# A reordered front of a fused attention kernel: index rows, corner tables and first one-hots

## The chip, the cores and the metric

The kernel runs on one core of a Trainium2 chip. The metric is the device time of one execution in microseconds (us); a smaller number is better. Engines are named as the profile names them: PE (TensorE matmul) and PEld (its weight load), DVE (VectorE), ACT (ScalarE), POOL (GpSimd) and SP (SyncE, which issues DMAs).

## What is computed

Eight layers run one after the other on `x` of shape (4, 16, 16, 32): a deformable attention (`L0`), a dynamic convolution, a causal attention, a mixture of experts, a linear attention and a spectral filter. The change touches `L0` and one weight product of the linear attention. Of `L0` this matters:

```python
qkv = x @ w_qkv + b_qkv
qkv = conv2d(qkv, w_dw, groups=3 * c) + b_dw            # 3x3, each channel by itself
off = conv1x1(pconv(q_img, pconv_off_w[i]), w_off[i], b_off[i])
py = rows + base_y + off[:, :, 0]; px = cols + base_x + off[:, :, 1]
y0, x0 = floor(py), floor(px)
out = gather(y0, x0) * (1 - wy) * (1 - wx) + gather(y0, x0 + 1) * (1 - wy) * wx + ...
attn = softmax(q . k_samples); out = attn . v_samples   # x is normalised ahead of all this
```

## The kernel before

`x` lies as 128 partitions (image, channel) x 256 tokens. The **front** normalises it (bn_stats, a power on POOL, `xg`), makes q, k and v by three products, and convolves them over nine taps: for q and k five taps on DVE and four on PE (diagonal weights), for v all nine on PE. From q come the offsets (`offsets_of`, three pairs of matmuls into PSUM).

**Index chain.** DVE adds offsets and `base` to `pos`, clamps it, rounds it to the corner `near` and multiplies row and column together into `index` (128 tokens x 288 points, bf16). PE turns `index` into rows (`turned_index`), ACT copies them (`idx_rows`, step "rows"), SP stores them to memory and loads them back broadcast over all partitions, a unit in four parts. A **unit** is 128 tokens of one image; there are T = 8, with J = 36 points each. Units 1 to 7 get their indices from memory. Unit 0 gets them by nine groups of four broadcast matmuls (`index_group`), each copied from PSUM to `indexb` by ACT.

**Tables.** `corner_tables(i)` transposes the four shifted copies of k (i = 0, 2) or v (i = 1, 3) into PSUM. Each table is split into three bf16 parts: ACT copies the high part (`table_high`), DVE subtracts (`table_rests`), ACT copies the middle (`table_mid`), DVE subtracts again (`table_low`). The v tables need the v convolution, which ACT copies out (step "vconv").

**Units.** For each unit DVE compares the indices with the partition number (`one_hots`), PE multiplies 36 x 2 x 3 = 216 times (128x64) a one-hot by a table part, ACT copies the samples out in five groups, and DVE does the attention (`keys`, `key_sums`, `value_sums` and small steps). From unit 1 on ACT makes a quarter of one half of the one-hots. `hats`, `mask_x` and `w4` are the interpolation weights, needed after unit 0's samples. Each engine runs its program in the order written; semaphore steps (`v0`, `a0`, `t0`, `g0`) name the waits. `occupied` issues matmuls on a tile of zeros, whose results are not used. `values_by_dense` are small products for a later layer, put ahead of units 5 and 7.

## Time and profile before

| | |
|---|---|
| runs | 208.39 us median of 3 (206.82 to 209.21) |
| the profiled execution | 208.35 us, of which 206.6 us is the span |
| mean granted clock of TensorE | 0.957 of full |
| PE, DVE, ACT, POOL busy | 181.7, 153.2, 97.8, 39.4 us |
| front, to unit 0's first matmul | 0 to 29.29 us of the span |
| the eight units on PE | 29.29 to 87.8 us |

The span runs from the first to the last instruction; times below are counted from its start. A timeline row gives start, length, engine, line, what is written and read, and in brackets the idle time before it and who ended it. Rows of several instructions give their count (x4); an fp32 matmul has two entries on PE.

### The profile page before, as it was taken

To read this page: it belongs to the slowest core of one execution; us is meant where nothing else is said; L and a number is where in the kernel's file an instruction comes from. 1 tells how busy PE (TensorE), PEld (TensorE's weight loads), DVE (VectorE), ACT (ScalarE), POOL (GpSimd) and SP (SyncE) were. 2 spreads that over 40 slices of the span, in tenths; PEclk is the share of its full clock that TensorE was granted. 3 is DMA by queue.
4 is the path that set the end of the run, shared out by engine and by line. 5 is a ranking of instruction groups with operands and counts; after the bars stand their busy time and mean duration, and the time that the engine had idled before them with its cause. 6 is when DMAs were issued, how large, how long until landed. Compare 5 with 4: busy or idle time off the path is not lost.

```text
span 206.6 us, 7009 instructions
## 1 busy us (share of the span) xinstructions
PE 181.7 (88%) x3060; PEld 138.2 (67%) x3068; DVE 153.2 (74%) x347; ACT 97.8 (47%) x240; POOL 39.4 (19%) x57
## 2 busy tenths in 40 slices
PE   7799989899879989986798899887999959978994
PEld 2677759899779989965244675343487728655972
DVE  2789998979999999789777266697987658647201
ACT  2743999589778769450102360121976510026200
POOL 5981000013421421450100300333000000110000
PEclk9999999999999999999999998899855899999999
DMA  6830345646445330000252140001210091000000
GB/s 197 293 115 2 83 164 157 191 155 192 157 143 172 132 107 3 8 0 9 65 146 76 28 112 3 0 5 35 69 25 3 3 202 21 0 0 3 3 0 25
DMA packets 9203, 16.03 MB, mean 78 GB/s; under 512 B 2536, under 2 KB 3912, under 8 KB 9044
## 3 DMA queue, kind: packets, MB, share of 16 engines
q1 hardware_dynamic: 9028, 15.28, 25.2%
q8 instruction: 24, 0.39, 0.8%
q10 hardware_dynamic: 144, 0.30, 0.4%
q14 instruction: 7, 0.06, 0.1%
HBM read 15.15 MB, written 0.42 MB: 75 GB/s over the span
## 4 chain that ended last, share of the span: by engine, by line
PE 65%; DVE 19%; ACT 6%; issue 5%; POOL 2%; DMA 2%; POOLq 1%; DVEq 0%
PE ps L1553 62%; POOL rstd L588 2%; DMA cst<-in_cst 2%; DVE stu_fq L1456 1%; ACT onehot L850 1%; ACT table L651 1%; DVE onehot L1083 1%; DVE arena L1537 1%; DVE arena L1063 1%; DVE att L1133 1%; ACT onehot L792 1%; DVE onehot L1405 1%; DVE comp L1418 1%; DVE table L1069 1%; ACT onehot L798 1%
## 5 line engine op out<-in xcount | busy, mean ns | idle before, releaser
L1553 PE MATMUL ps<-table,onehot 128*128 128x64 bf16 x1728 | 52.9, 193 | 4.7 <-issue 3.4
L1553 PEld LDWEIGHTS ps<-table,onehot 128*128 128x128 bf16 x1728 | 51.3, 98 | 6.3 <-issue 5.7
L1553 PE MATMUL ps<-spare 128*128 128x512 bf16 x97 | 28.7, 419 | 5.0 <-ACT onehot L651 1.4
L735 ACT ACTIVATE arena<-ps 128x512 f32<-128x512 f32 (+1 forms) x40 | 21.5, 553 | 13.9 <-PE ps L1553 13.8
L460 POOL TENSOR_TENSOR arena<-arena,w4p 128x288 f32<-128x288 f32 x21 | 16.3, 806 | 56.0 <-DVE arena L460 55.8
L588 POOL TENSOR_TENSOR rstd<-var_eps,cst 128x4 f32<-128x4 f32 (+2 forms) x9 | 8.8, 983 | 78.1 <-DVE var_eps L952 54.3
L651 ACT ACTIVATE arena<-ps 128x512 f32<-128x512 f32 (+4 forms) x17 | 7.3, 466 | 32.7 <-PE ps L1553 25.4
L1553 PE MATMUL ps<-arena 128*32 128x66 f32 (+6 forms) x388 | 22.6, 286 | 0.2 <-DVE arena L1333 0.2
L1553 PEld LDWEIGHTS ps<-arena 128*32 128x32 f32 (+3 forms) x388 | 18.7, 152 | 4.2 <-issue 1.6
L1553 PEld LDWEIGHTS ps<-spare 128*128 128x128 bf16 x105 | 9.9, 107 | 16.7 <-issue 4.4
L1083 DVE TENSOR_SCALAR onehot<-indexb,cst 128x2304 bf16<-128x2304 bf16 (+1 forms) x24 | 17.7, 770 | 0.0
L441 DVE TENSOR_TENSOR arena<-arena,q_tok 128x1152 f32<-128x1152 f32 x8 | 10.8, 1351 | 3.6 <-ACT arena L735 3.6
L651 ACT ACTIVATE indexb<-ps 128x128 f32<-128x128 f32 (+1 forms) x9 | 2.8, 325 | 19.6 <-PE ps L1850 15.7
L1553 PE MATMUL ps<-onehot,indexb 32*128 32x512 f32 x32 | 10.9, 805 | 0.4 <-ACT indexb L651 0.4
L1109 DVE TENSOR_REDUCE dots<-arena 128x144 f32<-128x1152 f32 x8 | 10.8, 1346 | 0.1
L1545 DVE SCALAR_TENSOR_TENSOR table<-ps,window,arena 128x128 f32<-128x128 f32 x2 | 0.6, 344 | 11.3 <-PE ps L1553 11.3
L798 ACT ACTIVATE onehot<-onehot,pos 128x1152 bf16<-128x1152 bf16 x7 | 8.8, 1251 | 0.0
L1553 PE MATMUL ps<-qkv_pad,arena 128*128 128x256 f32 x34 | 8.1, 381 | 0.0
L749 ACT ACTIVATE pexp<-logit,peak 128x9 f32<-128x9 f32 x28 | 8.1, 299 | 0.0
L1133 DVE TENSOR_REDUCE att<-arena 128x32 f32<-128x1152 f32 x6 | 8.1, 1342 | 0.0
L1553 PE MATMUL ps<-arena,cst 128*128 128x216 f32 (+4 forms) x38 | 6.9, 335 | 0.0
L1456 DVE SCALAR_TENSOR_TENSOR stu_fq<-stu_fq,ps 128x512 f32<-128x512 f32 x8 | 5.0, 682 | 2.6 <-ACT stu_fq L885 2.6
(280 smaller groups left out, 322.2 us busy)
## 6 DMA issues: line engine op xcount, KB each, us to landing
indexb<-index_rows SPq DMA_DIRECT2D x20, 288.0 KB, 3.4
stu_fq<-index_rows SPq DMA_DIRECT2D x8, 288.0 KB, 3.5
arena<-in_toep SPq DMA_DIRECT2D x2, 514.0 KB, 6.0
l<-in_l SPq DMA_DIRECT2D x1, 646.5 KB
stu_fq<-in_stu SPq DMA_DIRECT2D x1, 560.0 KB, 3.7
onehot<-in_l3w SPq DMA_DIRECT2D x1, 512.0 KB
table<-stu_mixed SPq DMA_DIRECT2D x4, 128.0 KB, 2.2
l<-in_l SPq DMA_DIRECT2D x1, 384.0 KB, 5.9
```

Source lines behind the costliest of these rows:

```text
L441: return engine.tensor_tensor(out=prod_k.rearrange("p (g n d) -> p g n d", g=G, d=HC), in0=samples(u, 0).rearrange("p (g s) (n d) -> p g ( ...
L460: ins = engine.tensor_tensor(out=out, in0=samples(u, 1).rearrange("p (g s) (d n) -> p g d s n", g=G, n=4)[:, g], in1=w[:, g].unsqueeze(1). ...
L588: nc.gpsimd.tensor_tensor(out=out_ap, in0=in_ap, in1=exponent, op=ALU.pow).then_inc(g0.sem, g0.step(name))
L651: nc.scalar.activation(out_ap, in_ap, ACT.Copy, scale=scale).then_inc(steps.sem, steps.step(name))
L735: nc.scalar.activation(gv[:, b % 2, :, at:at + count, :], ps[:, SB[n % len(SB)], 0:count * SLOT].rearrange("p (s a d) -> p a s d", s=count ...
L749: ins = nc.scalar.activation(pexp[:, g * K2:(g + 1) * K2], logit[:, g * K2:(g + 1) * K2], ACT.Exp, scale=-1.0, bias=peak[:, g:g + 1], accu ...
L798: nc.scalar.activation(ohv[:, u % 2, 1, J - OWN:, :], ohv[:, u % 2, 1, J - OWN:, :], ACT.Relu, bias=pos1[:], scale=-1.0).then_inc(s_os, 1)
L1083: ins = nv.tensor_scalar(ohv[:, u % 2, q, js, :], ixb[u % 3][:, js, :], c["pidx"][:, q:q + 1], None, ALU.is_equal)
L1109: nv.reduce_sum(dots[:], prod_k.rearrange("p (n d) -> p n d", d=HC), axis=AX.X)\
L1133: nv.reduce_sum(tokhb(att[:])[:, h, b, :], prod_v[u % 2].rearrange("p (n k) -> p n k", k=4 * K2), axis=AX.X)\
L1456: nv.scalar_tensor_tensor(out=features, in0=features, scalar=1.0, in1=by_query(ps[:, i % 4, :]), op0=ALU.min, op1=ALU.max).then_inc(v5.sem ...
L1553: return nc.tensor.matmul(out_ap, lhsT, rhs, start=start, stop=stop)
```

## The change

Line numbers shift by a few lines between the two files. The input `cst` (identity, base grid, constants) is issued by SP after `x` and `front`, no longer by ACT. DVE's four small steps on `cst` move away from the program's start. The power on POOL takes its exponent from a memset tile. `base` holds the grid less 0.5; `pos` is no longer clamped in place; two steps (clip, round) give `corner`, and PE multiplies rows by 16 and adds columns while it turns them. The nine `index_group`s are gone: unit 0's indices are loaded from memory in four quarters, ahead of unit 1's, and its one-hots are made a quarter at a time. PE has the offsets ahead of k's last two taps, turns the rows ahead of the k tables, and has seven of v's taps behind these. The v tables' remaining parts come ahead of unit 0's one-hots; ACT makes both hats. The dense products of unit 7 move to unit 6.

```diff
             sp.dma_start(front[:], front_d).then_inc(d_front, 16)
+            sp.dma_start(cst[:], cst_d).then_inc(d_cst, 16)
...
-            for u in range(1, T):
+            for u in range(T):
...
+            pool_e.wait_ge(v0.sem, v0["eps"])
+            power(rstd[:, 0:1], var_eps[:, 0:1], nhalf[:], "rstd0")
             pool_e.wait_ge(d_cst, 16)
-            power(rstd[:, 0:1], var_eps[:, 0:1], c["neghalf"][:, 0:1], "rstd0")
...
-            act.dma_start(cst[:], cst_d).then_inc(d_cst, 16)
...
+            act.wait_ge(t0.sem, t0["rows"])
+            copy(idx_rows[:], turned_index, a0, "rows")
             table_high(0)
             table_high(2)
             act.wait_ge(v0.sem, v0["gate"])
             nc.scalar.activation(gate_m[:], gate_m[:], ACT.Exp, scale=-1.0).then_inc(a0.sem, a0.step("sigexp"))
-            act.wait_ge(t0.sem, t0["rows"])
-            copy(idx_rows[:], turned_index, a0, "rows")
...
-            index_group(0)
             table_mid(0)
             table_mid(2)
...
+            distance(hat0, phalf, "hat0a")
             act.wait_ge(t0.sem, t0["vconv"])
...
+            nv.tensor_scalar(near, pos, 0.0, H - 2.0, ALU.max, ALU.min).then_inc(v0.sem, v0.step("clip"))
+            dve.wait_ge(v0.sem, v0["clip"])
+            nv.tensor_scalar(corner[:], near, ROUND, -ROUND, ALU.add, ALU.add).then_inc(v0.sem, v0.step("near"))
...
-            pe.wait_ge(v0.sem, v0["index"])
-            pe.wait_ge(a0.sem, a0["qtok"])
-            for k in range(3):
-                ins = nc.tensor.transpose(turned_index[:, k * P:(k + 1) * P], index[:, k * ROWS:(k + 1) * ROWS], identb[:])
+            pe.wait_ge(v0.sem, v0["near"])
+            by_axis = corner[:].rearrange("p (n a) -> p a n", a=2)
+            for k in range(3):
+                mm(turned_index[:, k * P:(k + 1) * P], by_axis[:, 0, k * ROWS:(k + 1) * ROWS], identw[:], stop=False)
+                ins = mm(turned_index[:, k * P:(k + 1) * P], by_axis[:, 1, k * ROWS:(k + 1) * ROWS], identb[:], start=False)
...
+            def first_one_hots(part):
+                js = slice(part * J // PARTS, (part + 1) * J // PARTS)
+                dve.wait_ge(d_quarter[part] if part < PARTS - 1 else d_ix[0], 16)
+                for q in range(2):
+                    ins = nv.tensor_scalar(ohv[:, 0, q, js, :], ixb[0][:, js, :], c["pidx"][:, q:q + 1], None, ALU.is_equal)
+                ins.then_inc(s_oh, 1)
...
-                elif u == 7:
-                    values_by_dense(2)
-                    values_by_dense(3)
...
                     rest_of(moe_ps, moe_raw[:], [moe3[:, t, :] for t in range(2)]).then_inc(tw.sem, tw.step("m2"))
+                    values_by_dense(2)
+                    values_by_dense(3)
```

On DVE, from the sum that makes `pos` to the first table subtractions (`ps` to `arena`, with `table`), the program before has:

```order
L1041 TENSOR_TENSOR arena<-ps,base_b 128x2x4x72 [waits tensor_front]
L1044 TENSOR_TENSOR gate_m<-ps,cst 128x2x4x9
L1048 TENSOR_SCALAR arena<-arena 128x576 [waits vector_front]
L1050 TENSOR_SCALAR arena<-arena 128x576 [waits vector_front]
L1052 TENSOR_SCALAR arena<-arena 128x576 [waits vector_front]
L1054 TENSOR_SCALAR arena<-arena 128x576 [waits vector_front]
L1057 SCALAR_TENSOR_TENSOR index<-arena 128x288 [waits vector_front]
L1063 TENSOR_TENSOR arena<-ps,table 128x512 [waits scalar_front] x2
```

and the changed program, from the three steps that were at the program's start:

```order
L1022 CAST identb<-cst 128x128
L1023 TENSOR_SCALAR identw<-cst 128x128
L1024 SCALAR_TENSOR_TENSOR base_b<-cst 128x144
L1033 TENSOR_TENSOR arena<-ps,base_b 128x2x4x72 [waits tensor_front,vector_front]
L1037 TENSOR_SCALAR arena<-arena 128x576 [waits vector_front]
L1039 TENSOR_SCALAR corner<-arena 128x576 [waits vector_front]
L1040 TENSOR_TENSOR gate_m<-ps,cst 128x2x4x9
L1045 TENSOR_TENSOR kv<-ps,kv 128x256 [waits vector_front,tensor_front]
L1051 TENSOR_TENSOR arena<-ps,table 128x512 [waits scalar_front] x2
```

Five steps behind `pos` became two, and k's last sum (L1045, before at L1035 and ahead of `pos`) now stands behind them.

On PE, from the last offsets to the v tables (`qkv_pad` with `arena` are convolution taps, `cst,kv` the table transposes), before:

```order
L1553 MATMUL ps<-arena 128x324 x3
L1598 MATMUL ps<-cst,kv 128x128 [waits vector_front]
L1598 MATMUL ps<-cst,kv 128x128 x7
L1553 MATMUL ps<-qkv_pad,arena 128x256 [waits pool_steps]
L1553 MATMUL ps<-qkv_pad,arena 128x256 x4
L1639 MATMUL ps<-identb,index 96x128 [waits scalar_front,vector_front]
L1639 MATMUL ps<-identb,index 96x128 x2
L1553 MATMUL ps<-identb,index 128x128 x4
L1553 MATMUL ps<-qkv_pad,arena 128x256 x4
L1553 MATMUL ps<-identb,index 128x128 x4
L1553 MATMUL ps<-spare 128x512 [waits scalar_front]
L1598 MATMUL ps<-cst,kv 128x128 [waits scalar_front]
```

and in the changed program:

```order
L1546 MATMUL ps<-arena 128x324 x3
L1546 MATMUL ps<-qkv_pad,arena 128x256 x2
L1546 MATMUL ps<-qkv_pad,arena 128x256 [waits pool_steps]
L1546 MATMUL ps<-qkv_pad,arena 128x256
L1546 MATMUL ps<-identw,corner 96x128 [waits scalar_front,vector_front]
L1546 MATMUL ps<-identb,corner 96x128
L1591 MATMUL ps<-cst,kv 128x128 [waits vector_front]
L1591 MATMUL ps<-cst,kv 128x128 x7
L1546 MATMUL ps<-qkv_pad,arena 128x256 x7
L1546 MATMUL ps<-spare 128x512 [waits scalar_front]
L1546 MATMUL ps<-spare 128x512
L1591 MATMUL ps<-cst,kv 128x128 [waits scalar_front]
```

The k tables (first `cst,kv` rows) stand behind the turned rows, which wait for the rounding; the broadcast groups are gone. The pair of `corner` matmuls comes three times; one pair is shown.

On DVE, from the k tables' low parts to the first one-hots, the program before has:

```order
L1069 TENSOR_TENSOR table<-arena,table 128x16x32 [waits scalar_front] x2
L1208 TENSOR_SCALAR arena<-arena 128x576 [waits vector_front]
L1063 TENSOR_TENSOR arena<-ps,table 128x512 [waits scalar_front] x2
L1213 TENSOR_SCALAR gate_m<-gate_m 128x72 [waits scalar_front]
L1215 RECIPROCAL gate_m<-gate_m 128x72 [waits vector_front]
L1217 COPY mask_x<-gate_m 128x288 [waits vector_front]
L1069 TENSOR_TENSOR table<-arena,table 128x16x32 [waits scalar_front] x2
L1083 TENSOR_SCALAR onehot<-indexb,cst 128x2304 [waits index_copied]
```

and the changed program, in the same stretch:

```order
L1057 TENSOR_TENSOR table<-arena,table 128x16x32 [waits scalar_front] x2
L1199 TENSOR_SCALAR gate_m<-gate_m 128x72 [waits scalar_front]
L1201 RECIPROCAL gate_m<-gate_m 128x72 [waits vector_front]
L1203 COPY mask_x<-gate_m 128x288 [waits vector_front]
L1051 TENSOR_TENSOR arena<-ps,table 128x512 [waits scalar_front] x2
L1057 TENSOR_TENSOR table<-arena,table 128x16x32 [waits scalar_front] x2
L1064 TENSOR_SCALAR onehot<-indexb,cst 128x1152 [waits first_index_loaded_0]
```

The three mask steps moved from between the v tables' two subtractions to ahead of both, and the one-hots are half as long each.

## Rows read from the trace of the kernel before

**Rows 1.** Chain that ended last, front: start us, us, what.
```profile
16.55 0.76 DVE arena L1041
...
19.33 0.47 DVE index L1057
...
22.26 0.48 ACT kv L718
...
27.68 1.47 DVE onehot L1083 x2
...
29.29 10.01 PE ps L1553 x334
```

**Rows 2.** Timeline of DVE, front and units.
```profile
4.14 0.19 DVE L976 TENSOR_SCALAR ahead<-cst 128x64 f32<-128x64 f32 x1 [3.00 <-DMA cst<-in_cst]
...
4.67 0.42 DVE L965 BATCH_NORM_STATS2 stats<-x 128x6 f32<-128x256 f32 x1
...
8.21 0.41 DVE L1005 TENSOR_SCALAR q_flat<-qkv_pad,front 128x256 f32<-128x256 f32 x1 [0.65 <-ACT qkv_pad L665]
...
15.92 0.42 DVE L1035 TENSOR_TENSOR kv<-ps,kv 128x256 f32<-128x256 f32 x1
...
17.85 0.46 DVE L1050 TENSOR_SCALAR arena<-arena 128x576 f32<-128x576 f32 x1
...
24.11 1.29 DVE L1063 TENSOR_TENSOR arena<-ps,table 128x512 f32<-128x512 f32 x2
...
43.56 1.36 DVE L441 TENSOR_TENSOR arena<-arena,q_tok 128x1152 f32<-128x1152 f32 x1 [1.09 <-ACT arena L735]
```

**Rows 3.** Timeline of PE, front.
```profile
6.85 1.53 PE L1553 MATMUL ps<-xg,front 128*128 128x256 f32 x6 [1.22 <-DVE xg L992]
...
16.40 1.09 PE L1598 MATMUL ps<-cst,kv 128*128 128x128 f32 x8
17.33 2.33 PE L1553 MATMUL ps<-qkv_pad,arena 128*128 128x256 f32 x10
```

**Rows 4.** DMA issues: tiles, count, KB each, median us from issue to landing.
```profile
indexb<-index_rows SPq DMA_DIRECT2D x20, 288.0 KB, 3.4
...
x<-in_x_ch SPq DMA_DIRECT2D x1, 128.0 KB, 3.2
...
index_rows<-idx_rows SPq DMA_DIRECT2D x1, 72.0 KB, 2.4
```

**Rows 5.** Timeline of SP: the first load, and the loads of unit 1's indices.
```profile
0.74 0.38 SPq L494 DMA_DIRECT2D x<-in_x_ch  x1
...
23.18 1.77 SPq L520 DMA_DIRECT2D indexb<-index_rows  x4
```

**Rows 6.** Timeline of ACT, front.
```profile
5.16 1.28 ACT L659 ACTIVATE arena<-cst,front 128x128 f32<-128x128 f32 x4 [2.50 <-DMA front<-in_front]
7.62 1.28 ACT L665 ACTIVATE qkv_pad<-ps,front 128x256 f32<-128x256 f32 x3 [1.18 <-PE ps L1553]
...
17.09 1.09 ACT L651 ACTIVATE table<-ps 128x512 bf16<-128x512 f32 x2 [3.16 <-PE ps L1598]
...
20.25 0.49 ACT L651 ACTIVATE idx_rows<-ps 96x384 bf16<-96x384 bf16 x1 [1.92 <-PE ps L1639]
...
28.84 0.84 ACT L756 ACTIVATE arena<-arena,neg 128x576 f32<-128x576 f32 x1
```

**Rows 7.** Groups by form, DVE one-hots: count, busy us, mean ns, idle.
```profile
L1083 DVE TENSOR_SCALAR onehot<-indexb,cst 128x1152 bf16<-128x1152 bf16 x1 | 0.5, 512 | 0.0
```

**Rows 8.** Timeline of PE, unit 6 and the products behind it.
```profile
74.61 5.88 PE L1553 MATMUL ps<-table,onehot 128*128 128x64 bf16 x196 [0.75 <-issue]
80.42 0.82 PE L1553 MATMUL ps<-l 32*32 32x32 f32 x32
```

**Rows 9.** Timeline of PE: the same products at the lower and higher clock.
```profile
156.94 3.75 PE L1553 MATMUL ps<-arena 128*32 128x66 f32 x128
...
162.40 2.05 PE L1553 MATMUL ps<-arena 128*32 128x66 f32 x128
```

More of the change, by code:

```diff
@@ L151, in hybrid @@
         mask_x = sb("mask_x", [P, T * J])
-        index = sb("index", [P, T * J], BF16)
+        corner = sb("corner", [P, 2 * T * J], BF16)
         table = sb("table", [P, 2 * 3 * B * G * SLOT], BF16)
@@ L265, in hybrid @@
             sem("loaded_" + n) for n in ("x", "cst", "front", "pw", "l1", "l2", "moe", "l3", "stu", "toep", "parity", "late", "out"))
-        v0 = Steps(sem("vector_front"), "spare neg1 pos1 ahead identb npidx base stats moments eps xg "
+        v0 = Steps(sem("vector_front"), "spare neg1 pos1 nhalf phalf stats moments eps xg "
                    + "qdiag " + " ".join(f"q{t}" for t in range(TAPS)) + " qsum k0 s20 s21 s30 s31 "
-                   + " ".join(f"k{t}" for t in range(1, TAPS)) + " ksum"
-                   + " pos gate clamp near0 near1 near index rest0 rest2 away hat0a low0 low2 hat0 rest1 rest3 gate1 sigmoid maskx"
-                   + " low1 low3 hatm w4")
-        a0 = Steps(sem("scalar_front"), "warm kdiag q k v comp s00 s01 s10 s11 qtok high0 high2 sigexp rows mid0 mid2 vconv"
-                   " high1 high3 mid1 mid3 hat1a hat1")
-        t0 = Steps(sem("tensor_front"), "q k v comp qconv select qtok kconv offsets table0 table2 rows vconv table1 table3")
+                   + " ".join(f"k{t}" for t in range(1, TAPS)) + " identb identw base"
+                   + " pos clip near gate ksum rest0 rest2 away low0 low2 gate1 sigmoid maskx"
+                   + " rest1 rest3 low1 low3 ahead npidx hatm w4")
+        a0 = Steps(sem("scalar_front"), "warm kdiag q k v comp s00 s01 s10 s11 qtok rows high0 high2 sigexp mid0 mid2 hat0a vconv"
+                   " high1 high3 mid1 mid3 hat0 hat1a hat1")
+        t0 = Steps(sem("tensor_front"), "q k v comp qconv select qtok offsets kconv rows table0 table2 vconv table1 table3")
         g0 = Steps(sem("pool_steps"), "qkvpad qpad stackpad kvpad xpad rstd0 vdiag bnvar bninv sigma "
@@ L285, in hybrid @@
         d_ix = tuple(sem(f"index_loaded_{i}") for i in range(3))
-        s_bc = sem("index_spread")
-        s_bce = sem("index_copied")
+        d_quarter = tuple(sem(f"first_index_loaded_{i}") for i in range(3))
         s_oh = sem("onehot_ready")
@@ L751, in unit_exp @@
                 ins.then_inc(s_px, 1)
-            for i in range(5, 9):
-                index_group(i)
-            act.wait_ge(v0.sem, v0["away"])
-            nc.scalar.activation(hat1, away, ACT.Abs, bias=neg1[:]).then_inc(a0.sem, a0.step("hat1a"))
-            act.wait_ge(a0.sem, a0["hat1a"])
-            nc.scalar.activation(hats.rearrange("p (n z) -> p n z", z=2)[:, :, 1], hat1, ACT.Relu,
-                                 bias=pos1[:], scale=-1.0).then_inc(a0.sem, a0.step("hat1"))
             def split(parts, t, src, name, done_by):
@@ L1080, in one_hots @@
                 for q in range(2):
-                    if q and half and u:
+                    if q and half:
                         js = slice(js.start, J - OWN)
@@ L1199, in _ @@
             table_rests(2)
-            nv.tensor_tensor(out=away, in0=pos, in1=near, op=ALU.subtract).then_inc(v0.sem, v0.step("away"))
-            dve.wait_ge(v0.sem, v0["away"])
-            nv.scalar_tensor_tensor(out=hat0, in0=away, scalar=-1.0, in1=away, op0=ALU.mult, op1=ALU.min).then_inc(v0.sem, v0.step("hat0a"))
+            dve.wait_ge(v0.sem, v0["near"])
+            nv.tensor_tensor(out=away, in0=pos, in1=corner[:], op=ALU.subtract).then_inc(v0.sem, v0.step("away"))
             table_low(0)
@@ L1613, in _ @@
             offsets_of(2, q_mid)
-            taps_of(1, ps[:, 4, N:2 * N], taps_k, TAPS, range(TAPS + 2, K2)).then_inc(t0.sem, t0.step("kconv"))
             pe.wait_ge(a0.sem, a0["s11"])
```

141 lines of the change are left out of this document (63 added, 78 removed).

## Prediction

> **What bounds the kernel now.** I read the views in this order: the chain of waits, the timelines of PE, DVE and ACT over the front, the issues of SP, and the units. The chain shows what to move: a front of 29.29 us that ends with the first unit's matmul [rows 1], then eight units in which PE is nearly full. DVE sat idle 1.09 us ahead of the second unit's `keys` [rows 2] and has no wait from there to unit 6's end, so PE and DVE are the bound together. Whatever the front gives, the units pass on one to one, as long as neither engine gets a new wait in them.
>
> Four stations of the front carry the sum: `pos` starts at 16.55, `index` is ready at 19.80, ACT starts the v convolution's copy at 22.26, and unit 0's first matmul starts at 29.29 [rows 1]. Behind the copy stand the v tables: their subtractions start at 24.11 [rows 2], 1.85 later; the first pair of one-hots starts at 27.68 and takes 1.47 [rows 1].
>
> **1. The front's start.** DVE starts bn_stats at 4.67, behind four steps on `cst`, which landed at 4.14 [rows 2]. PE starts its first product 2.18 later, at 6.85 [rows 3]. `x`, issued at 0.74, took 3.2 us to land [rows 4, 5], so it was there at 3.94. With the four steps moved, bn_stats can start when `x` lands; the power no longer needs `cst`. If `x` lands as before, that is 0.73 earlier. It no longer shares the transfer engines with `cst`, so I take 3.55, and PE's first product at 5.73, 1.12 earlier. ACT caps this: its diagonals started at 5.16, when `front` had landed, and took 1.28, to 6.44; it then copies q, before at 7.62, 0.77 behind PE's start [rows 6]. `cst` is now third in SP's queue. The bytes ahead of `l1` are the same three inputs, so I expect them all by about 5.1, and ACT copies q at about 6.5: 1.1 earlier. DVE's wait of 0.65 ahead of q's taps [rows 2] covers the small steps that now stand there. **Gain 1.1**, bounds 0.7 (`x` as before) and 1.2 (ACT's end at 6.44).
>
> The Trainium skill speaks against half of this: DMA: Bandwidth & Descriptors, section "Issuing engines are not separate DMA queues", says that transfers started from several engines run on the same 16 DMA engines and interleave, and that issuing from several only saves the issue time. Taken strictly, the order of issue would not bring `x` sooner, the gain would be 0.7, and the end 0.4 later than I forecast. No row of before has `x` ahead of `cst`.
>
> Below I count in the old clock of the front and subtract 1.1 at the end.
>
> **2. To `near`.** k's last DVE tap ends at about 15.85, since `ksum` starts at 15.92 [rows 2]. `ksum` gives way to three of the four moved steps (`identb`, `identw`, `base`); the four took 0.53 together [rows 2], so three take 0.4 to 0.5, and `pos` starts at about 16.36. The offsets no longer wait behind two of k's taps on PE; each tap costs 0.43 (ten entries from 17.33, 2.33 us [rows 3]), and they end before that. `pos` takes 0.76 [rows 1]; the two remaining steps start 0.49 apart (17.85 to 18.34) as those before [rows 2]. `corner` is ready at 16.36 + 0.76 + 0.98 = 18.1, where `index` took until 19.80: 1.7 less.
>
> **3. Turned rows and k tables.** PE turns the rows at 18.15; three transposes and their wait took 0.45 up to ACT's copy at 20.25 [rows 1, 6]. Six matmuls: 0.45 if the weights load as fast, 0.9 if twice as long; I take 0.6. ACT copies from 18.75 to 19.25. Meanwhile DVE makes `gate` and `ksum` (0.42 [rows 2]) to 18.6. So the k tables, before at 16.40 [rows 3], come at 18.65: **2.25 later**. Here the index step has moved ahead of the tables on all three engines.
>
> **4. To the v copy.** The tables hold PE for 0.93 (16.40 to 17.33 [rows 3]). Then seven v taps: 14 entries at 0.217 and a last one's 0.38 give 3.2, to 22.8. On ACT, k's high parts (0.55 each [rows 6]) start 0.69 behind the tables, at 19.35, and end at 20.45; DVE's two subtractions (0.64 each [rows 2]) end at 21.2 and `away`, as wide as `pos`, at 21.95; ACT's `distance` takes 0.84 [rows 6], to 22.8. PE and ACT arrive together, and the v copy starts at 22.83, **0.57 later** than 22.26. Before, ACT came to it late, behind an index group and two middle parts; now PE's taps come late.
>
> **5. From the v copy to the first matmul.** As before, 1.85 to the v subtractions: 24.68. The two end at 25.97. ACT's last middle part takes 0.55 to 0.6, DVE's last low part 0.64: 27.3. Before, that was 27.68. The three mask steps, which filled the 1.0 us between the v subtractions' end at 25.40 and two low parts of 0.64 ahead of 27.68, go into DVE's wait for ACT ahead of 24.68, and no index group cuts into ACT. The first quarter's two one-hots take half of 1.47, or 2 x 0.51 as the one of that length [rows 7]: 0.75 to 1.0, I take 0.9. First matmul: 27.25 + 0.9 + 0.14 = 28.3. In the new clock 27.2, against 29.29: **2.1 earlier**.
>
> **6. Indices through memory.** ACT's copy ends at 19.25 - 1.1 = 18.15. Store 2.4, load 3.4 [rows 4]: the first quarter at 24.0. Four issues took 1.77 [rows 5], so the fourth goes out 1.3 later and lands at 25.3, or later if the four share the engines. DVE is ready for the first at 26.15 and for the fourth 2.7 later. So the path through memory costs nothing while it stays under the tables; its cover is 2 us for the first quarter. Unit 1's four loads go out 1.8 behind and are needed at about 30.
>
> **7. Inside the units.** DVE's eight half-length one-hots take 3.7 instead of 3.0, and two small steps 0.25; unit 0's weights and unit 1's one-hots end about 0.5 later relative to PE. The 1.09 wait ahead of 43.56 [rows 2] takes that. ACT makes both hats, 2.5 us, ahead of its first samples, and meets them about when they are ready. Nothing lost, bound 0.5 lost.
>
> **8. The dense products.** 0.82 us leave the place ahead of unit 7 [rows 8] and enter ahead of unit 6. PE works from unit 5 to unit 7 without waiting for DVE; its 0.75 inside unit 6 [rows 8] falls 20 matmuls in, where no semaphore stands. A serial engine ends at the same time whichever of its two units holds them. **0**; 0.75 gained if that stall is slack that the products fill.
>
> **Sum.** Span 206.6 - 2.1 = 204.5. The profiled execution was 208.35, 1.75 over its span, so 206.25; the median is 208.39, the same within 0.04. **Forecast 206.2 us.** Its own range is 205.5 to 206.9: 0.4 for the front's start, 0.3 for the row matmuls and half one-hots.
>
> **The rivals.** (a) *The start gives only its short end, or the units take back some.* `x` as before costs 0.4, `cst` third in line another 0.3 through ACT's diagonals, the lost cover of step 7 up to 0.5: 206.6 to 207.6. For it: nothing shows `x` alone on the engines. Chance 0.27.
> (b) *DVE paces the last units, and the products fill slack.* 0.75 more, with `x` sooner: 204.6 to 205.5. For it: DVE is gapless there. Against it: PE is, too. Chance 0.15.
> (c) *The memory path ends last.* It decides from 2 us of extra landing on. For it: eight loads go out back to back where four did. Against it: the first has the engines to itself. 206.5 to 208. Chance 0.06.
> (d) *Slower: TensorE's clock falls in the front.* Before, it was granted in full up to here, with PE idle 1.22 us ahead of its first product [rows 3] and filled up by zero matmuls. The new order takes three of these and all broadcast matmuls away, and PE waits for `corner`, for `ksum` and for ACT. The same 128 products took 3.75 us at the lower and 2.05 at the higher clock [rows 9], 1.8 times. At that rate the seven taps and both tables (4.6 us) cost 3.7 more, and unit 0 (216 matmuls, 6.5 us by the 196 in 5.88 of [rows 8]) up to 5.2 more: 210, and up to 213. It makes the kernel slower from 2.1 us lost. Against it: the estimated gaps are under 1 us, as before. Chance 0.05.
>
> **How the numbers follow.** Forecast 0.47, (a) 0.27, (b) 0.15, (c) 0.06, (d) 0.05. A measurement of this kernel tells about 1% from no change, which puts the line at 206.3. Faster by over 1%: the forecast's better half (0.3), all of (b) and a little of (a): 0.5. Slower by over 1%: (d), 0.05. Within 1%: 0.45. The range 204.6 to 207.7 leaves (d), the end of (c), and a tail below out. Later stretches at the lower clock fall where PE's gaps put them, another reason not to be narrower.
>
> **What would show it.** bn_stats at about 3.5; `pos` about 1.3 earlier than 16.55; two steps to `corner`; the k tables *later* than `ksum` allows, behind the turned rows; the v copy waiting for PE; DVE's first one-hot right behind the last table part, with no wait for a load; the first matmul at about 27.2. A wait for a load there means (c), a granted clock under full in the front (d), unit 7 starting earlier than the shift (b). If bn_stats starts at 3.9, the first term was too large.

## The result, and the profile after

The changed kernel takes **205.65 us** (median of 22 runs, 204.26 to 208.71) against 208.22 before (22 runs). The ratio is 0.9867 with a 95% interval of 0.9842 to 0.9891: faster by 1.3%. The forecast was 206.2 us in a range of 204.6 to 207.7. The total came out well; two of its terms did not, and their errors have opposite signs. The changed kernel's profiled execution was disturbed in its late part (span 206.2 us), so below only what lies ahead of 88 us is compared with before; there the units end 2.69 us earlier, as much as the difference of 2.57 between the medians within the spread of the runs.

VectorE (DVE) of the changed kernel, by its timeline (start us, us, engine, line, operation, out<-in, count, idle ahead and what ended it):

```profile
2.87 0.43 DVE L960 BATCH_NORM_STATS2 stats<-x 128x6 f32<-128x256 f32 x1 [1.71 <-DMA x<-in_x_ch]
...
5.76 0.99 DVE L982 TENSOR_SCALAR arena<-cst,front 128x128 f32<-128x128 f32 x4 [0.97 <-DMA cst<-in_cst]
...
7.51 0.44 DVE L994 TENSOR_SCALAR q_flat<-qkv_pad,front 128x256 f32<-128x256 f32 x1 [0.31 <-ACT qkv_pad L664]
...
15.75 0.76 DVE L1033 TENSOR_TENSOR arena<-ps,base_b 128x576 f32<-128x576 f32 x1
...
17.04 0.46 DVE L1039 TENSOR_SCALAR corner<-arena 128x576 bf16<-128x576 f32 x1
...
25.43 1.29 DVE L1057 TENSOR_TENSOR table<-arena,table 128x512 bf16<-128x512 f32 x2
26.64 3.52 DVE L1064 TENSOR_SCALAR onehot<-indexb,cst 128x1152 bf16<-128x1152 bf16 x8
...
32.30 2.70 DVE L1075 TENSOR_SCALAR onehot<-indexb,cst 128x2304 bf16<-128x2304 bf16 x4
35.85 1.36 DVE L442 TENSOR_TENSOR arena<-arena,q_tok 128x1152 f32<-128x1152 f32 x1 [0.85 <-ACT arena L737]
...
41.78 1.35 DVE L442 TENSOR_TENSOR arena<-arena,q_tok 128x1152 f32<-128x1152 f32 x1
...
79.70 1.35 DVE L442 TENSOR_TENSOR arena<-arena,q_tok 128x1152 f32<-128x1152 f32 x1
```

These answer to [rows 2] and to the stations of [rows 1]. The moments of `x` start at 2.87 instead of 4.67, but q's taps only at 7.51 instead of 8.21: between them stand the diagonals, which begin when `cst` lands, at 5.76. `pos` starts at 15.75 (16.55), `corner` at 17.04, the last table parts at 25.43, and the first one-hots follow them without a wait for a load. The wait of 1.09 that stood ahead of unit 1's key products in [rows 2] is gone (41.78); the last row is unit 6's key products.

TensorE (PE), same view, with unit 0's first matmul, its three pauses ahead of 53 us ("issue": no semaphore held it), and the first matmul behind unit 7:

```profile
4.93 1.53 PE L1546 MATMUL ps<-xg,front 128*128 128x256 f32 x6
...
18.03 1.09 PE L1591 MATMUL ps<-cst,kv 128*128 128x128 f32 x8
...
27.73 15.14 PE L1546 MATMUL ps<-table,onehot 128*128 128x64 bf16 x499 [1.08 <-DVE onehot L1064]
43.11 3.91 PE L1546 MATMUL ps<-table,onehot 128*128 128x64 bf16 x128 [0.24 <-issue]
47.39 3.97 PE L1546 MATMUL ps<-table,onehot 128*128 128x64 bf16 x127 [0.37 <-issue]
52.28 3.37 PE L1546 MATMUL ps<-table,onehot 128*128 128x64 bf16 x110 [0.92 <-issue]
...
78.67 6.46 PE L1546 MATMUL ps<-table,onehot 128*128 128x64 bf16 x216 [0.52 <-ACT arena L737]
84.97 2.74 PE L1546 MATMUL ps<-arena,cst 128*128 128x216 f32 x16
```

The k tables come at 18.03, 1.63 *later* than in [rows 3], behind the turned rows, as the change orders it; unit 0 starts at 27.73 instead of 29.29, 1.56 earlier. The units end at 84.97. Before they ended at 87.66, by these rows of the same view of the kernel before, and of DVE's:

```profile
40.06 9.61 PE L1553 MATMUL ps<-table,onehot 128*128 128x64 bf16 x314 [0.76 <-issue]
...
61.96 3.40 PE L1553 MATMUL ps<-table,onehot 128*128 128x64 bf16 x111 [1.05 <-issue]
...
87.66 2.74 PE L1553 MATMUL ps<-arena,cst 128*128 128x216 f32 x16
```

```profile
27.60 3.00 DVE L1083 TENSOR_SCALAR onehot<-indexb,cst 128x2304 bf16<-128x2304 bf16 x4
...
36.45 1.36 DVE L441 TENSOR_TENSOR arena<-arena,q_tok 128x1152 f32<-128x1152 f32 x1 [1.01 <-ACT arena L735]
...
81.46 1.35 DVE L441 TENSOR_TENSOR arena<-arena,q_tok 128x1152 f32<-128x1152 f32 x1
```

ScalarE (ACT) and the loads of the changed kernel: its timeline, its DMA issues in the first 9 us (tiles, queue, count, KB, us from issue to landing), and SP's issues of the index loads:

```profile
6.94 1.18 ACT L664 ACTIVATE qkv_pad<-ps,front 128x256 f32<-128x256 f32 x3
...
22.19 0.47 ACT L721 ACTIVATE kv<-ps,front 128x256 f32<-128x256 f32 x1
...
32.17 1.26 ACT L787 ACTIVATE onehot<-indexb,npidx 128x1152 bf16<-128x1152 bf16 x1 [0.84 <-DMA indexb<-index_rows]
```

```profile
cst<-in_cst SPq DMA_DIRECT2D x1, 288.5 KB, 4.1
...
x<-in_x_ch SPq DMA_DIRECT2D x1, 128.0 KB, 2.1
```

```profile
21.87 3.68 SPq L521 DMA_DIRECT2D indexb<-index_rows  x8
```

`x` took 2.1 us to land instead of 3.2 [rows 4], `cst` 4.1 instead of 3.4, and it was issued third. The v copy starts at 22.19 (22.26 in [rows 1]). The eight first index loads go out from 21.87 on; the last of them, unit 1's, landed at 32.17, where ACT had waited 0.84 for it.

### The profile page after: what moved, and what is told of

Same layout as the page of the kernel before. It is cut to its first block, busy times and chain, and to the rows that moved or that the text cites. A ratio compares the mean times of both kernels' runs of the same rounds, so it can differ in the third digit from the quotient of the medians.

```text
span 206.2 us, 6936 instructions
## 1 busy us (share of the span) xinstructions
PE 182.9 (89%) x3023; PEld 136.7 (66%) x3031; DVE 151.6 (74%) x349; ACT 95.4 (46%) x233; POOL 39.2 (19%) x57
## 4 chain that ended last, share of the span: by engine, by line
PE 69%; DVE 17%; ACT 6%; issue 4%; POOL 1%; POOLq 1%; DVEq 0%
PE ps L1546 66%; POOL rstd L589 1%; DVE stu_fq L1449 1%; DVE q_flat L997 1%; ACT onehot L845 1%; PE ps L1591 1%; DVE arena L475 1%; ACT arena L650 1%; DVE arena L1530 1%; DVE table L1057 1%; DVE att L1125 1%; ACT onehot L787 1%; ACT table L650 1%; DVE onehot L1398 1%; DVE comp L1411 1%
## 5 line engine op out<-in xcount | busy, mean ns | idle before, releaser
L1546 PE MATMUL ps<-spare 128*128 128x512 bf16 x93 | 28.3, 440 | 4.8 <-DVE rexp L1365 1.4
L589 POOL TENSOR_TENSOR rstd<-var_eps,cst 128x4 f32<-128x4 f32 (+2 forms) x8 | 8.3, 1035 | 78.3 <-DVE var_eps L947 56.2
L1075 DVE TENSOR_SCALAR onehot<-indexb,cst 128x2304 bf16<-128x2304 bf16 (+1 forms) x20 | 14.7, 763 | 0.0
L1546 PE MATMUL ps<-onehot,indexb 32*128 32x512 f32 x32 | 12.3, 941 | 0.6 <-ACT indexb L650 0.6
L1443 DVE TENSOR_SCALAR arena<-ps,cst 128x512 f32<-128x512 f32 x8 | 6.0, 747 | 1.8 <-ACT arena L650 1.8
L1546 PEld LDWEIGHTS ps<-qkv_pad,arena 128*128 128x128 f32 x34 | 6.3, 189 | 1.5 <-issue 0.6
```

The source lines that it names most:

```text
L589: nc.gpsimd.tensor_tensor(out=out_ap, in0=in_ap, in1=exponent, op=ALU.pow).then_inc(g0.sem, g0.step(name))
L1075: ins = nv.tensor_scalar(ohv[:, u % 2, q, js, :], ixb[u % 3][:, js, :], c["pidx"][:, q:q + 1], None, ALU.is_equal)
L1443: nv.tensor_scalar(vcv[:, t, :, :, D:2 * D], ps[:, VBANK[t], :].rearrange("p (g r n) -> p g r n", g=HG, r=4), c["cs"][:, 2 * h + 1:2 * h + ...
L1546: return nc.tensor.matmul(out_ap, lhsT, rhs, start=start, stop=stop)
```

## The experiments

Three stations are compared in all runs: the start of q's taps on DVE, unit 0's first matmul, and the end of the units (the start of the first matmul behind unit 7). A fourth number is the stretch from DVE's key products of unit 1 to the end of the units, in which nothing of the front is left. Each number is read from the timeline of that run.

| kernel | x's moments | q's taps | first matmul | units' end | keys(1) to end | ratio to before (95%) |
|---|---|---|---|---|---|---|
| before | 4.67 | 8.21 | 29.29 | 87.66 | 44.10 | 1 |
| changed | 2.87 | 7.51 | 27.73 | 84.97 | 43.19 | 0.9867 (0.9842 to 0.9891) |
| cst_on_act | 3.89 | 7.88 | 29.22 | 86.29 | 43.24 | 0.987 (0.978 to 0.996) |
| cst_on_act_12 | 3.91 | 7.38 | 27.52 | 84.55 | 43.46 | 0.990 (0.986 to 0.995) |
| before_start | 2.89 | 7.87 | 29.02 | 87.05 | 43.53 | none |
| before_start_9 | 2.87 | 7.37 | 28.59 | | | none |
| store_twice | 2.82 | 7.43 | 28.10 | 87.03 | 43.29 | 0.999 (0.995 to 1.002) |
| dense_back | 2.85 | 7.53 | 27.75 | 84.83 | 43.18 | 0.989 (0.980 to 0.998) |
| before_dense | 4.57 | 8.11 | 29.20 | 87.36 | 43.84 | 0.997 (0.992 to 1.002) |
| before_small_loads | 4.65 | 8.19 | 29.27 | 87.02 | 43.20 | 0.998 (0.993 to 1.003) |
| shifted | 2.92 | 7.57 | 27.78 | 85.74 | 44.32 | 0.987 (0.982 to 0.991) |
| q_first | 2.80 | 6.58 | 26.77 | 84.00 | 43.18 | 0.986 (0.979 to 0.994) |
| q_first_again | 2.84 | 6.55 | 26.74 | 83.79 | 43.17 | 0.985 (0.980 to 0.990) |
| q_ident | 2.84 | 6.81 | 27.19 | 84.85 | 43.16 | 0.988 (0.984 to 0.992) |

Most of the differences are under 1 us of 206, and the intervals of the times are 0.5 to 2% wide. What tells the theories apart is the stations. For before_start and before_start_9 there is no ratio, and of before_start_9 only the front is used, since its unit 5 took 8.02 us, with the granted clock lower for a part of it, where other units take about 6.5.

### The start: which load holds q's taps

Theory 1: step 1 of the prediction gained 0.7 and not 1.1 because `cst`, third in one queue, landed late. First undone alone:

```diff
-            sp.dma_start(cst[:], cst_d).then_inc(d_cst, 16)
+            act.dma_start(cst[:], cst_d).then_inc(d_cst, 16)
```

> The changed kernel with one edit: the constants cst are issued on ACT's queue again, as in the kernel before, so that x and front stand alone on SP's queue. Theory 1 (the front's start gained 0.7 us and not 1.1 because cst, third in SP's queue, landed at 5.76): cst lands between 4.1 and 5.1, the copy of q starts near 6.5 instead of 6.94, VectorE's q taps near 7.1 instead of 7.51, the first unit's matmul near 27.3 instead of 27.73, and the time falls by about 0.4 us. Rival: x lands later when cst travels beside it from another queue (the moments at 3.2 or later instead of 2.87), the normalized input xg comes later by as much, and the time is the same or up to 0.3 us longer.

DVE and PE of this kernel, by the timeline:

```profile
3.89 0.43 DVE L961 BATCH_NORM_STATS2 stats<-x 128x6 f32<-128x256 f32 x1 [2.73 <-DMA x<-in_x_ch]
```

```profile
6.01 2.90 PE L1547 MATMUL ps<-xg,front 128*128 128x256 f32 x6 [0.81 <-DVE xg L976]
...
29.22 10.98 PE L1547 MATMUL ps<-table,onehot 128*128 128x64 bf16 x371 [1.07 <-DVE onehot L1065]
```

The rival held in part: with `cst` travelling beside it, `x` came 1.02 later. But the first matmul came 1.49 later, and that has a second cause: the six products of the start took 2.90 us, where the changed kernel's took 1.53 (the last section has why). With the 12 spare matmuls of before in place of 9, the two are apart:

> The changed kernel with cst on ACT's queue and 12 spare matmuls, both as before. With 9 the six products of the start took 2.90 us instead of 1.53 behind a gap of 0.81, so that run mixed two things. Theory (x comes 1.0 later beside cst, and the rest of its loss of 1.49 was the slow products): first product near 5.9, six products in about 1.5, ACT's diagonals done at 6.5, q's copy near 6.5 and its taps near 7.1 to 7.3, first matmul 27.3 to 27.6, a little ahead of the changed kernel's 27.73: the two orders of the loads then differ by under 0.4 us. Rival (x late is what costs): q's taps at 7.8 or later and the first matmul at 28.0 or later.

PE of this kernel, by the timeline, with the six products and unit 0's first matmul:

```profile
6.03 1.53 PE L1547 MATMUL ps<-xg,front 128*128 128x256 f32 x6
...
27.52 10.89 PE L1547 MATMUL ps<-table,onehot 128*128 128x64 bf16 x368 [1.07 <-DVE onehot L1065]
```

The products took 1.53 again, and the first matmul came at 27.52, 0.21 ahead of the changed kernel. So the order of the loads only chooses which of them is late: `x` early and `cst` late, or the reverse. Either way q's taps start at about 7.4 to 7.5. The prediction had taken the early `x` of the one order and the early `cst` of the other together.

The start's edits alone, on the kernel before (`cst` third on SP's queue, the exponent by memset, the small DVE steps moved):

> The kernel before with the edits of the start alone: cst third on SP's queue, the exponent of the normalization as a memset, the small VectorE steps on cst moved behind; the index path, the order of the tables and the dense products as before. Forecast's step 1: q's taps on VectorE start 1.1 us earlier than 8.21 and the first unit's matmul 1.1 earlier than 29.29. Theory 1, corrected by the changed kernel's trace (cst lands near 5.76): q's taps 0.7 earlier, first matmul 28.5 to 28.7. Rival: the moved steps come back as time ahead of the corner, and the first matmul gains under 0.4. The time follows with 0.7 us (207.5 against 208.2), or less where TensorE's pauses in the units fall worse.

PE of that kernel, by the timeline:

```profile
6.28 1.77 PE L1555 MATMUL ps<-xg,front 128*128 128x256 f32 x6
```

The same with 9 spare matmuls:

> The kernel before with the edits of the start and with 9 spare matmuls ahead of the first product instead of 12, as the change has them. With 12 the spare matmuls held TensorE until 6.28 though the normalized input was there at 4.81, and q's taps started at 7.87. Theory (start and shorter warm-up belong together): first product near 4.9, q's taps near 7.45 (ACT's diagonals behind cst end at 6.96 and hold q's copy), first matmul 28.5 to 28.7. Rival (the products run slower without the longer warm-up and take back what is gained): q's taps still near 7.5, but the query sum later than 10.3 and the first matmul at 28.8 or later.

PE of this one, by the timeline:

```profile
5.00 2.15 PE L1555 MATMUL ps<-xg,front 128*128 128x256 f32 x6
...
28.59 9.99 PE L1555 MATMUL ps<-table,onehot 128*128 128x64 bf16 x337 [0.86 <-DVE onehot L1083]
```

Alone, the start gains 0.27 at the first matmul, as little as the rival had said, but not for its reason: the normalized input was there at 4.81 (DVE's step on it starts at 4.40 and takes 0.41), but PE was still in its 12 spare matmuls until 6.28. With 9 it gains **0.70**. What the changed kernel has beyond that, 28.59 to 27.73, is the new order of the tables and the index path: **0.86**.

### The index path: how much cover it has

```diff
             sp.wait_ge(d_rows, 16)
+            sp.dma_start(rows_d.rearrange("(k r) n -> r k n", k=3), idx_rows[:].rearrange("r (k n) -> r k n", k=3)).then_inc(d_rows, 16)
+            sp.wait_ge(d_rows, 32)
```

> The changed kernel with one thing doubled: the store of the index rows is issued and waited for a second time ahead of the index loads, which makes the way through memory about 3.2 us longer. Forecast's step 6 (the way is covered by about 2 us, behind the tables' second half): the one-hots of unit 0 wait for the first load and start 0.8 to 1.5 us later than 26.64, and the first matmul comes 1 to 1.9 later than 27.73. Rival (the way has 3 us or more to spare): no change before unit 1. Rival (c) of the forecast (the way is what ends last already): 3.2 us later.

SP and DVE of this kernel, by the timeline:

```profile
23.81 3.67 SPq L523 DMA_DIRECT2D indexb<-index_rows  x8
```

```profile
27.00 2.76 DVE L1066 TENSOR_SCALAR onehot<-indexb,cst 128x1152 bf16<-128x1152 bf16 x6 [0.35 <-DMA indexb<-index_rows]
30.10 0.95 DVE L1066 TENSOR_SCALAR onehot<-indexb,cst 128x1152 bf16<-128x1152 bf16 x2 [0.34 <-DMA indexb<-index_rows]
...
34.13 2.71 DVE L1077 TENSOR_SCALAR onehot<-indexb,cst 128x2304 bf16<-128x2304 bf16 x4 [0.86 <-DMA indexb<-index_rows]
```

The loads went out 1.94 later (23.81 against 21.87), since the second store took less than the first's 3.2. Ahead of unit 0, DVE waited only 0.35, less than the 0.8 to 1.5 expected: there the way through memory is covered by about 1.5 us, as step 6 had it, if with less than its 2. But the end of the units moved by 2.06, more than the whole delay. Later waits do it: 0.34 at 30.10 for unit 0's last quarter, and most of all 0.86 at 34.13, for *unit 1's* load. In the changed kernel that load landed at 32.17 and DVE wanted it at 32.30: a cover of 0.13. So the cover was worked out for the wrong unit. Eight loads of 288 KB share the transfer engines: in the changed kernel the quickest of them took 3.3 us to land and the slowest 7.0. The first lands in time with a margin, the eighth just in time. Rival (c) of the prediction decides from 0.13 us of extra landing on, not from 2.

### The units: dense products or pauses

The changed kernel's units gained 1.13 beyond the earlier first matmul (2.69 less 1.56), where steps 7 and 8 said 0. Two candidates: the dense products in another place (theory 2), or TensorE's pauses (theory 3). The dense products put back, and the dense products moved in the kernel before:

```diff
+                elif u == 7:
+                    values_by_dense(2)
+                    values_by_dense(3)
...
-                    values_by_dense(2)
-                    values_by_dense(3)
```

> The changed kernel with one edit: the dense products of the values stand at unit 7 again, behind unit 6's samples, as in the kernel before. Theory 2 (ahead of unit 6's samples they lie in time in which TensorE waits for one-hots anyway): unit 7's end comes 0.4 to 0.9 us later than 84.97 with VectorE's row as before to unit 6's samples, and the time rises by as much. Rival (TensorE does them one after the other wherever they stand, 0.82 us for two): units end at 84.97 within 0.2 and the time is the same; the units' gain then came from elsewhere, for instance from where TensorE's own stalls fall.

> The kernel before with one edit: the dense products moved from unit 7 to unit 6, as the change has them. Forecast's step 8 (TensorE lags behind the one-hots there, so that the products cost the same in both places): units end at 87.66 within 0.2, no gain. Theory 2 in its strong form (they fill slack there too): units end 0.5 to 0.8 earlier and the time falls by 0.5 to 0.8 us. The changed kernel's gain of 0.93 in unit 6 and 7 would then be the dense products' alone; with no gain here it needs the missing lag of TensorE as well.

PE of dense_back, by the timeline:

```profile
70.89 6.46 PE L1546 MATMUL ps<-table,onehot 128*128 128x64 bf16 x216 [0.57 <-DVE onehot L1075]
...
78.53 6.46 PE L1546 MATMUL ps<-table,onehot 128*128 128x64 bf16 x216 [0.44 <-DVE onehot L1075]
84.83 2.74 PE L1546 MATMUL ps<-arena,cst 128*128 128x216 f32 x16
```

Undoing the move cost nothing (84.83 against 84.97), and the move alone in the kernel before gave 0.26 in the last stretch, with a shorter pause in unit 6. The reason stands in the rows: PE *waits for one-hots* in units 6 and 7, and of the 0.82 us of dense products most lies inside such a wait in either place. Theory 2 falls; step 8's 0 was right for a reason that step 8 did not give.

The pauses, with the index loads of units 3 to 7 cut to a ninth in the kernel before:

```diff
+                    js = js if u < 3 else slice(js.start, js.start + 1)
```

> The kernel before with the index loads of units 3 to 7 cut to a ninth of their rows; these units then work on indices left from an earlier unit, so the numbers of their samples are not the reference's. Work and instructions on the engines stay. Theory 3 (TensorE's pauses of 0.4 to 1 us without a wait, one for some 256 instructions of its stream, last as long as they do because the broadcast loads of the indices, 16 engines for several us, hold up its instructions): the pauses in units 3 to 7 shrink below 0.4 us each, units end 0.8 us or more ahead of 87.66, and the time falls by as much. Rival: the pauses stay as they are (0.5 to 1 us at the same instruction numbers), and the time is the same within 0.3 us.

PE of this kernel, by the timeline, in unit 1 and at the start of unit 4:

```profile
40.32 9.34 PE L1554 MATMUL ps<-table,onehot 128*128 128x64 bf16 x314 [0.76 <-issue]
...
57.80 6.46 PE L1554 MATMUL ps<-table,onehot 128*128 128x64 bf16 x216 [0.76 <-DVE onehot L1084]
```

In unit 1, whose loads were whole, the pause of 0.76 stands as in the kernel before. Behind it there is none: from unit 4 on PE waits for DVE in each unit, and the last stretch takes 43.20 instead of 44.10. That is DVE's own pace, since the changed kernel (43.19), dense_back (43.18) and q_first (43.18) have the same number. The time did not follow clearly (0.998, with 1 in the interval); 0.64 us at the units' end (0.8 or more were expected) are 0.3%.

Then the place of the pauses, moved by 51 matmuls:

```diff
-            occupied_after(v0, ("spare", 9), bank=7)
+            pe.wait_ge(v0.sem, v0["spare"])
+            for _ in range(30):
+                mm(ps[:, 7, 0:P], spare[:, 0:P], spare[:, 0:P])
...
-            occupied_after(a0, ("high1", 3), ("high3", 3), ("mid1", 2), ("mid3", 2), bank=7)
+            for name, n in (("high1", 12), ("high3", 12), ("mid1", 8), ("mid3", 8)):
+                pe.wait_ge(a0.sem, a0[name])
+                for _ in range(n):
+                    mm(ps[:, 7, 0:P], spare[:, 0:P], spare[:, 0:P])
```

> The changed kernel with the spare matmuls of the front cut into more, smaller ones (30 of 128 columns for 9 of 512, and 40 for 10), so that every later matmul of TensorE has another number in its stream, by about 51. Theory 3 (TensorE pauses at fixed numbers of its stream, about every 128 matmuls, and how long is set by the loads that run beside it): pauses fall 51 matmuls earlier in the units (after 448 matmuls of the units instead of 499, and so on by 128), units end between 84.8 and 85.6, later than 84.97 where a long pause meets unit 6 or 7. Rival: the pauses hang on the data or on banks and stay at 499, 627 and 754. The front may be slower by what the smaller matmuls leave of TensorE's clock; the units are to be read from their own start.

PE of this kernel, by the timeline, with the count of matmuls up to each pause:

```profile
27.78 13.43 PE L1546 MATMUL ps<-table,onehot 128*128 128x64 bf16 x448 [1.06 <-DVE onehot L1064]
42.70 7.61 PE L1546 MATMUL ps<-table,onehot 128*128 128x64 bf16 x255 [1.49 <-issue]
50.66 3.89 PE L1546 MATMUL ps<-table,onehot 128*128 128x64 bf16 x128 [0.34 <-issue]
...
85.74 2.74 PE L1546 MATMUL ps<-arena,cst 128*128 128x216 f32 x16
```

The rows count the matmuls between pauses: 448, then 255, then 128. In the changed kernel it is 499, 128, 127. 499 less 51 is 448, and from there both pause again some 128 or 256 matmuls on. So pauses hang on the number of the instruction, not on the data. Here one of 1.49 fell early in unit 2, the last stretch took 44.32, and the units ended 0.77 later than the changed kernel's with the same front. That is two thirds of the 1.13 that the changed kernel had gained in the units.

### A further step: ACT copies q first

The start's rows show what holds q's taps: ACT makes four diagonals (1.28 us, behind `cst`) ahead of q's copy, which needs only `front`. q_first swaps them and moves the three small selection steps from ahead of q's taps into DVE's wait for ACT's table copy, and ACT's exponential of the selection behind the v copy. The diff shows the swap alone.

```diff
-            act.wait_ge(d_cst, 16)
             act.wait_ge(d_front, 16)
-            for t in range(TAPS, K2):
-                ins = nc.scalar.activation(taps_k[:, (t - TAPS) * P:(t - TAPS + 1) * P], ident, ACT.Copy,
-                                           scale=f["wdw"][:, K2 + t:K2 + t + 1])
-            ins.then_inc(a0.sem, a0.step("kdiag"))
             act.wait_ge(g0.sem, g0["qkvpad"])
             for j, (name, src) in enumerate((("q", ps[:, 0, 0:N]), ("k", ps[:, 1, 0:N]), ("v", ps[:, 4, 0:N]))):
+                if j == 1:
+                    act.wait_ge(d_cst, 16)
...
+                    ins.then_inc(a0.sem, a0.step("kdiag"))
```

> The changed kernel, further changed: ACT copies q ahead of the four diagonals for k (it waited for cst there, and q's copy needs only front), and the three small VectorE steps of the selection and ACT's exponential behind them move from ahead of q's taps into times in which these engines wait later in the front. Theory: the copy of q at 5.3 to 5.6 instead of 6.94, q's taps on VectorE right behind its diagonals at 6.8 instead of 7.51, the corner 0.7 earlier than 17.04, first matmul near 27.0, and the time 0.4 to 0.8 us shorter than the changed kernel's. Rival: TensorE's taps or ACT's comp copies, now behind k and v, end last ahead of the query sum, and the gain is under 0.3.

> The kernel of run q_first again, unchanged, for a closer time: ratio to before 0.982 to 0.985, where the changed kernel has 0.9867, if its units end 0.97 earlier as its trace shows and nothing behind them gives that back. Rival: the tail behind the units gives it back, and the ratio is 0.986 to 0.988.

ACT and PE of the first of the two runs, by the timeline:

```profile
5.65 0.48 ACT L666 ACTIVATE qkv_pad<-ps,front 128x256 f32<-128x256 f32 x1 [3.43 <-PE ps L1548]
6.03 1.27 ACT L662 ACTIVATE arena<-cst,front 128x128 f32<-128x128 f32 x4
```

```profile
26.77 15.15 PE L1548 MATMUL ps<-table,onehot 128*128 128x64 bf16 x499 [1.07 <-DVE onehot L1066]
```

q's taps started 0.93 earlier than the changed kernel's, and all of it came through: the first matmul 0.96, the units' end 0.97 earlier (1.18 in the second run, with its spans at 202.9 and 202.4). By the stations it beats both kernels. The time says it less surely: medians of 205.04 and 204.90 against 205.65, and ratios of 0.986 and 0.985 whose intervals overlap that of the changed kernel.

One more, with the identity of `cst` loaded as a part of its own behind `front`:

```diff
-            sp.dma_start(cst[:], cst_d).then_inc(d_cst, 16)
+            sp.dma_start(cst[:, 0:P], cst_d[:, 0:P]).then_inc(d_ident, 16)
+            sp.dma_start(cst[:, P:], cst_d[:, P:]).then_inc(d_cst, 16)
```

> The run q_first, further changed: cst is loaded in two parts, first the identity (64 KB) right behind front, then the rest, and the diagonals wait for the identity alone. Theory: VectorE's diagonals start near 5.2 instead of 5.66, q's taps right behind ACT's copy of q (5.65 to 6.13) near 6.2, first matmul near 26.4, and the time 0.3 us or so below q_first's. Rival: the identity with rows of 512 bytes takes as long as all of cst, or the rest of cst comes late for a later step, and nothing is gained.

PE and DVE of this kernel, by the timeline:

```profile
5.00 2.07 PE L1552 MATMUL ps<-xg,front 128*128 128x256 f32 x6
```

```profile
4.67 0.87 DVE L987 TENSOR_SCALAR arena<-cst,front 128x128 f32<-128x128 f32 x4
6.81 0.45 DVE L993 TENSOR_SCALAR q_flat<-qkv_pad,front 128x256 f32<-128x256 f32 x1 [1.27 <-ACT qkv_pad L668]
...
29.11 0.95 DVE L1070 TENSOR_SCALAR onehot<-indexb,cst 128x1152 bf16<-128x1152 bf16 x2 [0.35 <-DMA indexb<-index_rows]
```

DVE's diagonals started 0.99 earlier than in q_first, but q's taps 0.23 later: the six products took 2.07 in this execution, ACT copied q late, and later DVE waited 0.35 for an index quarter. Nothing was gained, and with that one slow stretch of products what the split load alone is worth stays open.

## Why the prediction was right, and where not

**Step 1 (start, 1.1 forecast) failed in size.** It measured 0.70, by before_start_9 and by q's taps in the changed kernel. `x` came even sooner than the 3.55 assumed (2.87), and the first product with it (4.93 against 5.73). What failed was the sentence that the three inputs would all be there by about 5.1: `cst` landed at 5.7. Rival (a) had named it: "`cst` third in line another 0.3 through ACT's diagonals". The step also did not say that the shorter warm-up was part of the gain (12 spare matmuls became 9, an edit that the diff of the change above does not show); without it 0.43 of the 0.70 are lost. As to the rule of the Trainium skill that stood against half of the step (DMA: Bandwidth & Descriptors, "Issuing engines are not separate DMA queues"): the runs agree that transfers from two engines interleave, since `x` took 3.1 us to land with `cst` beside it (cst_on_act) and 2.1 ahead of it in the same queue. My reading, that the order of issue would then not matter, was wrong.

**Steps 2 to 5 (the new order, 1.0 forecast) held.** In the clock of the old front (0.70 added): `pos` 16.45 (16.36 forecast), the k tables 18.73 (18.65), the v copy 22.89 (22.83), the first matmul 28.43 (28.3). Their sum measured 0.86 between before_start_9 and the changed kernel. The k tables came later, as said, and the v copy still moved little. One reading of step 2 was wrong without harm: `identw` is not one of the four moved steps but a new one, and the three steps ahead of `pos` took 0.67 (15.08 to 15.75), not 0.4 to 0.5.

**Step 6 (index path) was right in its result and wrong in its margin.** No DVE instruction waits for an index load, but the cover is 0.13 us at unit 1, and 1.5 at unit 0. Two terms were too small: the store took 3.2 us and not 2.4, and of the eight loads the last took 7.0 to land where the step had 3.4. store_twice showed that 1.94 more on this way cost 2.06 at the end.

**Step 7 (inside the units, 0) failed, on the good side.** The units gained 1.13 relative to the first matmul. Between DVE's first one-hots and its key products of unit 1 the time fell from 15.96 (43.56 less 27.60) to 15.14 (41.78 less 26.64): the waits of 1.01 and 1.09 became 0.85 and nothing, while the eight shorter one-hots and two small steps added about 0.5. Behind that, 0.91: the last stretch fell from 44.10 to DVE's own 43.2. From unit 2's key products to unit 6's DVE takes 7.64 us a unit in both kernels, without a wait (to 81.46 before, to 79.70 now), so the 0.91 lies wholly behind them: PE ended unit 7 6.20 us after them before and 5.27 now. In the kernel before the pauses of 0.76 inside unit 1 and of 1.05 and 0.75 in units 4 and 6 had put PE behind DVE; in the changed kernel the first ones fall behind unit 1, and even the 0.92 in unit 3 ends inside PE's slack. The prediction had read [rows 2] as both engines being the bound; it is DVE, and PE only where a pause makes it late. Rival (b), "DVE paces the last units", was right on that and wrong on the dense products.

**Step 8 (dense products, 0)** held; see dense_back.

**The sum** of 2.1 was thus 1.56 from the front and 1.13 from the units. Two errors of -0.5 and +1.1 left the forecast 0.55 too high. That it came so near is in part luck: the start gave less than was said, the units more, and the two errors cancel in part.

Rival (d), a lower clock in the front, did not come in the changed kernel's profiled execution: its six products took 1.53 us and its table transposes 1.09, as in [rows 3], and the granted clock is 1.00 from 4.68 us to the end of the units. At the very start it did come in variants with the same nine spare matmuls (last section), and cst_on_act, where it came, has its first matmul 1.70 later than cst_on_act_12, where it did not.

Not settled: how the gain in the units splits between the change and the luck of instruction numbers. From the first matmul to the units' end, the changed kernel and six variants (store_twice and shifted left aside) took 57.03 to 57.66 us, and before, before_start and before_dense 58.03 to 58.37; so the gain repeats. But in all seven the pauses fall at the same places of the stream, give or take 3 matmuls. shifted alone moves them, with the same work and the same front, and took 57.96: of the 1.13, 0.4 is left there, while its ratio (0.987) is that of the changed kernel.

## What to carry to other kernels

Cover is to be worked out for the last transfer of a burst that shares the engines, not for the first, and for each unit that waits on it. When a load is moved, look at what stands in line behind the *latest* load on each engine; here an in-order ScalarE held a copy that needed only an earlier one, and swapping the two was worth more than any order of the loads. Where two engines look like the bound together, take the stretch behind the front by itself: the number that stays the same over many variants is the pace of the one that sets it.

## What was not expected of the hardware

TensorE pauses without a semaphore at fixed places of its stream, 128 matmuls apart or a multiple of it, 0.2 to 1.5 us long. The profile's DMA part lists an instruction queue of its own (q8: 24 packets, 0.39 MB in the whole run, so 16 KB each):

```profile
q8 instruction: 24, 0.39, 0.8%
```

The page of the kernel before counts 3060 matmuls on PE, one packet for every 127.5. The packet records of the traces show what a pause waits for (us from the span's start):

| kernel | packet of q8 | pause | from the packet's end to the pause's end |
|---|---|---|---|
| before | 37.61 to 38.59 | 39.30 to 40.06 | 1.47 |
| before | 59.60 to 60.55 | 60.91 to 61.96 | 1.41 |
| changed | 49.92 to 50.85 | 51.36 to 52.28 | 1.43 |
| shifted | 40.29 to 41.25 | 41.21 to 42.70 | 1.45 |

All 53 pauses that the timelines of the fourteen traces show in the units end 1.21 to 1.53 us behind the end of such a packet, so a pause is the wait for a late packet of instructions. That the index loads make it late is what before_small_loads says: there seven packets between 53 and 78 us started about 0.4 to 1.2 us after PE had passed such a place of its stream, and in the kernel before seven packets between 50 and 76 us about 1.1 to 2.7 after; the four that started latest stand ahead of its four pauses in units 3 to 6. This is one execution of each kernel. That pauses vanish is not enough by itself: q_ident and cst_on_act_12, with whole loads, show none in units 4 to 7 either; PE waits for DVE ahead of most of these units, and a packet that comes within such a wait costs nothing.

The six products of the start took 1.53 us in some executions and longer in others, behind the same nine spare matmuls: 1.53 in the changed kernel, dense_back and both runs of q_first, 2.07 in q_ident, 2.15 in before_start_9, 2.44 in store_twice, 2.90 in cst_on_act. The profile's column of the granted clock says 1.00 in all of them, but the clock records of a trace begin only where the clock is full: at 3.84 to 4.68 us in the four with 1.53, ahead of the first product, and at 6.19 to 9.53 in the four others, among the products or behind them. Ahead of that moment matmuls of one length start 0.43 us apart, and 0.21 behind it, so TensorE ran there at the lower of its two levels. Where `cst` held ACT, long products cost q's taps nothing in before_start_9 (7.37) and store_twice (7.43); where ACT copies q first, as in q_ident, they are paid. With twelve spare matmuls the products took 1.53 in four kernels (before, before_dense, before_small_loads and cst_on_act_12), and 1.77 in before_start, where the records begin at 6.90. What decides the moment is open.
